# Three edits to a fused attention and feed-forward kernel: who adds up the probabilities and when, where GpSimd's bias goes, and a last tile in halves

## The chip, the cores and the metric

The kernel runs on one core of a Trainium2 chip. The metric is the device time of one execution in microseconds; the time of a kernel is the median of several runs. The engines are TensorE (PE, with its weight loads as PEld), VectorE (DVE), ScalarE (ACT), GpSimd (POOL) and SyncE (SP), which here only issues transfers.

## The reference

A block of a vision-language model for 4 batches of 512 tokens with 512 channels, and a context of 1024 tokens. Cut to what matters:

```python
def block(x, cond):                      # x (4,512,512), cond (4,1024,512)
    h = layernorm(x)
    q = qdq(h) @ qdq(wq).T + bq          # qdq: symmetric int8 rounding per row
    k, v = split(cond @ wkv.T + bkv)     # 16 heads of 32
    attn = softmax(q @ k.T / sqrt(32))
    o = attn @ v
    x = x + tanh(g_xattn) * (qdq(o) @ qdq(wp).T + bp)
    h = layernorm(x)
    f = silu(h @ gate_w * gs) * (h @ up_w * us)      # 1536 wide, weights fp8-rounded
    return x + tanh(g_ffn) * (f @ down_w * ds)
```

## The kernel before

All engines run their own written-out instruction lists and meet at semaphores. The kernel goes through the batches in four passes, b = 0 to 3.

The attention of a pass has 4 groups of 4 heads, and a group has 8 units, each of 128 context tokens for all 512 queries (`UNITS` is 32). A unit is: `scores` on TensorE (four matmuls, L1469), two exponentials on ScalarE (L836, two heads each), `values` on TensorE (four matmuls, L1486). The denominator of the softmax is a sum of the probabilities over all context tokens. In passes 1 to 3 the units named in `ADDED` (L157) are added up by VectorE (`add_unit`, two adds a unit, L1080) into `acc`; the first add of a group takes two units' probabilities, so seven units cost twelve adds. The units that are not named are summed by TensorE (`sums`, L1500). At the end of a group TensorE takes the finished `acc` in `totals` (L1514), which waits for the last add and stands in TensorE's list behind the first scores of the next group and ahead of all others. The next group's first add waits until `totals` has read `acc`. ScalarE may be three units ahead of the adds (`P_RING`).

Beside the adds VectorE prepares the next batch's x in steps, a generator `x_ahead` (L981) of which one step is taken ahead of the adds of each unit in `AHEAD_UNITS` (L136). Its order for passes 1 and on: four statistics (L958, one a tile), one aggregation (L964, L966), four normalisings (L969), four largest magnitudes (L935), the scales and four scalings (L944), four roundings (L950). `x_ahead(2)` runs in pass 1, `x_ahead(3)` in pass 2. The x itself is loaded at L536, when the gate and up products of the pass before are done.

GpSimd puts the bias of the projection on the residual in `residual_bias` (L666), four operations of 128x512; in passes 1 to 3 it does so behind the inverse deviation for the next x. VectorE wants the result ahead of the eviction of the projection (L1234).

Behind the attention ScalarE copies the denominator out of PSUM (L846, semaphore `den_out`) and the last group's output (L847). TensorE turns the denominator and the outputs; VectorE takes reciprocals (L1214) and multiplies (L1222, PSUM by `rden` into `r1`), finds magnitudes (L935), scales and rounds. Projection, second layernorm and the feed-forward part follow. In passes 0 and 1, steps for the next pass's score maxima are placed beside the down product: the last of them (`("S", G - 1, 0)`) stands ahead of the eviction of the last tile, `DOWN3`, and ends in VectorE's `crow` operation (L1047).

The down product has four tiles a pass. A tile is 24 matmuls of 512 columns (`down_step`, L1504); VectorE evicts it with the scale (L1155) and adds it to the residual (L1158, `down_tile`), and SyncE stores it (`store_rows`, L529). In the last pass nothing follows.

SyncE brings the stacked keys and queries of groups 2 and 3 (`stack`, 12 transfers each, L517, and `shift_row`, L527), started when the scores of the group before the last one are done.

Of the kernel before, what the change touches and what calls it, by code (L numbers as in the profile page):

```python
# [125 lines left out]
CHAIN_LATE = (CHAIN_LAST[0:5] + ["LATE1"] + CHAIN_LAST[5:13] + ["LATE2", "LATE3"] + CHAIN_LAST[13:])  # L126

LATE_EARLY = 8
D_SEQ = [CHAIN + HI_SEQ + ffn_seq(b) for b in range(B - 1)] + [CHAIN_LATE + ffn_seq(B - 1)]
D_BANK = [{n: k % 8 if k < len(CHAIN) else FREE_RING[(k - len(CHAIN)) % 4] for k, n in enumerate(seq)}  # L130
          for seq in D_SEQ[:B - 1]]
# [1 line left out]
_banks = (0, 1, 2, 3, 4, 5, 7, 0, 1, 2, 3, 4, 5, 7, 6)  # L133
D_BANK.append({n: _banks[k] if k < len(_banks) else (k + 1) % 8 for k, n in enumerate(D_SEQ[B - 1])})

AHEAD_UNITS = ((3, 5, 7, 18, 20) + tuple(range(22, 30)), tuple(range(1, 6)) + tuple(range(8, 25)))  # L136
STREAM0 = [s for n in A_SEQ0 for part in STEPS0.get(n, []) for s in part] + LEAD0 + UNIT_LIST0
assert [s for s in STREAM0 if s[0] == "D"] == DIFFS
STREAM0 = [s for s in STREAM0 if s[0] in "RSW"]
# [14 lines left out]
P_RING = (2, 3)  # L154


ADDED = ((0, 1, 2, 3, 4, 5, 6), (0, 1, 2, 4, 5, 6), (0, 1, 2, 4, 5, 6), (0, 1, 2, 3, 4, 5, 6))  # L157
ADD_HEADS = 2
ADD_PARTS = HG // ADD_HEADS
ADD_UNITS = [g * MT + t for g in range(G) for t in ADDED[g][1:]]  # L160
# [115 lines left out]
def pair_count(b, u, j):  # L276

    return b * 2 * UNITS + 2 * u + j // 2 + 1


class Steps:
# [14 lines left out]
def build(nc, ctxT, x, wq, wkvT, wp, gate_w, up_w, down_w, bqT, bkT, bv, bp, gsT, usT, ds,  # L296
          g_x, g_f, out):
    with ExitStack() as ctx:
# [177 lines left out]
        def _(sp):  # L476
# [52 lines left out]
            def store_rows(b, tiles):  # L529
                rows = out[b].rearrange("(t p) c -> p t c", p=P)  # L530
                for t in tiles:
                    sp.wait_ge(x_done, b * NT + t + 1)
                    sp.dma_start(rows[:, t, :], residual(b, t)).then_inc(stored, 16)

# [23 lines left out]
            for b in range(B):  # L558
# [43 lines left out]
                else:  # L602
                    store_rows(b - 1, LATE)
                    store_rows(b, range(NT))
            sp.wait_ge(stored, B * NT * 16)


        @block.gpsimd
        def _(pool):
# [32 lines left out]
            def inverse_deviation(n):  # L642
                pool.wait_ge(var_ready, n)
                nc.gpsimd.tensor_tensor(rstd[:, :], mv[:, :, 1], mhalf[:, :], ALU.pow).then_inc(rstd_ready, 1)  # L644
# [51 lines left out]
            for b in range(B):  # L696
                if b == 0:
                    first_units()
                else:
                    if b < B - 1:  # L700
                        inverse_deviation(variance_of_x(b + 1))
                    residual_bias(b)
                inverse_deviation(variance_of_x2(b))
                ahead = b + 2 < B
                if ahead:
                    pool.wait_ge(d_full, d_full_count(b, "K7"))
                    for c in range(CHUNK_BUFFERS[b + 2]):
                        load_ctx(b + 2, c)
                for i in range(FT):
                    pool.wait_ge(f_hi, b * FT + i + 1)  # L710
                    nc.gpsimd.tensor_tensor(f2_at(b, 1, i), fus[:, i % 2, :], f2_at(b, 0, i),  # L711
                                            ALU.subtract).then_inc(f_ready, 1)
                    if ahead and i in CHUNKS_BY_GATES[b]:
                        chunk(b + 2, CHUNKS_BY_GATES[b].index(i))
                for c in range(len(CHUNKS_BY_GATES[b]) if ahead else CHUNKS, CHUNKS):
                    chunk(b + 2, c)
# [188 lines left out]
        def _(dve):  # L905
# [277 lines left out]
            for b in range(B):  # L1183
                last = b == B - 1

                ahead = x_ahead(b + 1) if not last else None
                for u in range(UNITS):
                    g, t = divmod(u, MT)
                    if b == 0:
# [102 lines left out]
                    beside(name)  # L1292
                if b == 0:
                    dve.wait_ge(w_done, W_STEPS)
                for t in range(NT):
                    name = f"DOWN{t}"
                    if name not in d_seq(b):
                        continue
                    beside(name)
                    down_tile(b, t, b, name)  # L1300


        @block.tensor
        def _(pe):
# [196 lines left out]
                                          prob[:, p_slot(b, u, j), :], start=(u == (MT - 1 if b else 0)), stop=(u == UNITS - 1))  # L1501
                mm.then_inc(p_used, 1)

            def down_step(b, out, t, i):  # L1504
                for part in range(2):
                    mm = nc.tensor.matmul(out, f2_at(b, part, i)[:, t * P:(t + 1) * P], w_down[:, i, :],  # L1506
                                          start=(i == 0 and part == 0), stop=(i == FT - 1 and part == 1))
                return mm

# [59 lines left out]
            for b in range(B):  # L1569
# [23 lines left out]
                for name in d_seq(b):  # L1593
                    out_bank = d_bank(b, name)
                    out = bank(out_bank)
                    kind = name.rstrip("0123456789") if name[:3] != "X2T" else "X2T"
                    n = int(name[len(kind):] or 0)
                    if kind == "TOP":
                        continue
                    ahead = [lambda part=part: [maxima(b + 1, s) for s in part] for part in AHEAD[b].get(name, [])]  # L1600

                    if name != "LATE2":
                        bank_free(b, name)
                    if kind == "LATE":
                        for i in range(LATE_EARLY if n == 2 else 0, FT):
                            mm = down_step(b - 1, out, n, i)
                        mm.then_inc(d_full, 1)
                        if n == 1:
                            bank_free(b, "LATE2")
                            for i in range(LATE_EARLY):  # L1610
                                down_step(b - 1, bank(d_bank(b, "LATE2")), 2, i)
                    elif kind == "V":
                        if n == 0:
                            pe.wait_ge(ctx_ready, (b + 1) * CHUNKS)
                        v_product(out, n, d_full)
                    elif kind == "DEN":
                        pe.wait_ge(den_out, b + 1)
                        turn(out, [denT[:, t * P:(t + 1) * P] for t in range(NT)], d_full)
                    elif kind == "O":
                        if n == 0:  # L1620
                            pe.wait_ge(o_out, (b + 1) * G)
                        turn(out, [oT[:, g, n * P:(n + 1) * P] for g in range(G)], d_full)
                    elif kind == "OQT":
                        if n == 0:
                            pe.wait_ge(oq_ready, (b + 1) * NT)
                        turn(bank(out_bank, dt=BF16), [oq[:, t, n * P:(n + 1) * P] for t in range(NT)], d_full)
                    elif kind == "PROJ":
                        if n == 0:
                            pe.wait_ge(oqt_copied, (b + 1) * CT)
                        pair(out, [(oqT[:, k, n * P:(n + 1) * P], wpT[:, k, :]) for k in range(CT)], d_full)  # L1630
                    elif kind == "SX":
                        pe.wait_ge(diag_ready, (b + 2) * NT)
                        scales_product(out, d_full)
                    elif kind == "XT":
                        if n == 0:
                            pe.wait_ge(xq_ready, (b + 2) * NT)
                        turn_x(out_bank, n, d_full)
                    elif kind == "X2T":
                        if n == 0:
                            pe.wait_ge(x2_ready, (b + 1) * NT)  # L1640
                        turn(out, [x2[:, t, n * P:(n + 1) * P] for t in range(NT)], d_full)
                    elif kind == "Q":
                        if n == 0:
                            pe.wait_ge(x_copied, (b + 2) * X_COPIES)
                        q_product(out, n, d_full)
                    elif kind == "K":
                        k_product(out, n, d_full, ahead)
                    elif kind == "GU":
                        i, k = divmod(n, 2)
                        if n == 0:  # L1650
                            pe.wait_ge(d_free, d_free_count(b, f"X2T{CT - 1}"))
                        if b == 0 and i % (WCH // P) == 0:

                            pe.wait_ge(w_done, w_at[("gate", "up")[k], CT - 1, i // (WCH // P)] + 1)
                        pair(out, [((w_gate, w_up)[k][:, c, i * P:(i + 1) * P], x2T[:, s, c, :])
                                   for c in range(CT) for s in range(2)], d_full)
                        for step in ahead:
                            step()
                    else:
                        for i in range(FT):  # L1660
                            if ahead and i in (DOWN_AT_LATE if b == B - 2 else DOWN_AT)[name]:
                                ahead.pop(0)()
                            if n == 0:
                                if b == 0:
                                    pe.wait_ge(w_done, w_at["down", i] + 1)
                                pe.wait_ge(f_ready, b * FT + i + 1)
                            mm = down_step(b, out, n, i)
                        mm.then_inc(d_full, 1)
# [37 lines left out]
```

## Time and profile before

| | |
|---|---|
| median of 3 runs | 938.24 us (937.95 to 938.37) |
| the profiled execution | 936.7 us |
| its span, first to last instruction | 934.9 us, mean granted clock 0.991 |
| busy, share of the span | PE 92%, DVE 72%, ACT 59%, POOL 27% |
| chain that ended last | PE 68%, DVE 13%, ACT 10%, issue 7%, DMA 1% |
| load of x, 1024 KB | 6.0 us from issue to landing |

The span leaves out 1.8 us of the execution's time that lie around the instructions. Matmuls are pipelined in the trace: one that starts before the other ended is not a contradiction, and a busy TensorE is no measure of its peak. In the timelines, "x4" merges four operations of a kind; the time is from the start of the first to the end of the last; the bracket gives the idle time of the engine ahead of it and the engine and line that ended it.

### The profile page before, as it was taken

To read this page: it belongs to the slowest core of one execution; us is meant where nothing else is said; L and a number is where in the kernel's file an instruction comes from. 1 tells how busy PE (TensorE), PEld (TensorE's weight loads), DVE (VectorE), ACT (ScalarE), POOL (GpSimd) and SP (SyncE) were. 2 spreads that over 40 slices of the span, in tenths; PEclk is the share of its full clock that TensorE was granted. 3 is DMA by queue.
4 is the path that set the end of the run, shared out by engine and by line. 5 is a ranking of instruction groups with operands and counts; after the bars stand their busy time and mean duration, and the time that the engine had idled before them with its cause. 6 is when DMAs were issued, how large, how long until landed. Compare 5 with 4: busy or idle time off the path is not lost.

```text
span 934.9 us, 13575 instructions
## 1 busy us (share of the span) xinstructions
PE 864.1 (92%) x5000; PEld 310.2 (33%) x5000; DVE 671.5 (72%) x1292; ACT 554.4 (59%) x693; POOL 256.7 (27%) x236
## 2 busy tenths in 40 slices
PE   5987888999899998999899998999999989998998
PEld 2421121124433331224433331224433322233443
DVE  6887968938676769876766679886867768678222
ACT  5546777562556657884356647885256678871330
POOL 1145789770017603000006713000001213000130
PEclk9998999999999999999999999999999999999999
DMA  9334244410111143200020133210020014200001
GB/s 332 97 89 128 84 125 116 127 46 1 43 32 46 40 125 96 51 2 1 17 58 24 50 109 97 49 32 1 4 48 1 1 46 111 54 1 23 12 1 45
DMA packets 37106, 55.28 MB, mean 59 GB/s; under 512 B 8944, under 2 KB 15152, under 8 KB 37040
## 3 DMA queue, kind: packets, MB, share of 16 engines
q1 hardware_dynamic: 35120, 48.13, 18.1%
q0 software_dynamic: 1920, 6.29, 2.3%
q8 instruction: 39, 0.64, 0.3%
q14 instruction: 27, 0.22, 0.1%
HBM read 31.21 MB, written 4.19 MB: 38 GB/s over the span
## 4 chain that ended last, share of the span: by engine, by line
PE 68%; DVE 13%; ACT 10%; issue 7%; DMA 1%; ACTq 0%; DVEq 0%
PE ps L1325 33%; PE ps L1469 9%; PE ps L1506 8%; PE ps L1486 8%; ACT r L836 5%; PE ps L1448 4%; DVE acc L1080 3%; PE ps L1500 2%; PE ps L1514 1%; PE ps L1309 1%; DVE kst L1055 1%; ACT xq L795 1%; ACT r L795 1%; ACT r L744 1%; DVE r L1222 1%
## 5 line engine op out<-in xcount | busy, mean ns | idle before, releaser
L836 ACT ACTIVATE r<-ps 128x1024 f32<-128x1024 f32 x256 | 251.4, 1022 | 74.1 <-PE ps L1469 71.7
L1469 PE MATMUL ps<-qst,kst 97*128 97x512 f16 x512 | 140.9, 387 | 15.4 <-ACT r L836 13.0
L1055 DVE CUSTOM_DVE_ANT_0 kst<-ps,kst 128x512 f32<-128x512 f32 x192 | 124.5, 686 | 30.3 <-PE ps L1448 28.4
L1486 PE MATMUL ps<-r,vv 128*32 128x512 f32 x1024 | 138.1, 612 | 3.4 <-ACT r L836 3.2
L1080 DVE TENSOR_TENSOR acc<-acc,r 128x1024 f32<-128x1024 f32 x108 | 129.8, 1258 | 3.5 <-ACT r L836 3.1
L795 ACT ACTIVATE kst<-ps 128x1024 f32<-128x1024 f32 x96 | 98.2, 1023 | 53.3 <-PE ps L1381 53.0
L644 POOL TENSOR_TENSOR rstd<-mv,mhalf 128x4 f32<-128x4 f32 x8 | 9.9, 1240 | 344.9 <-DVE mv L966 344.9
L1325 PE MATMUL ps<-xs,w_gate 128*128 128x512 f16 x384 | 91.0, 380 | 1.5 <-DVE xs L1260 1.5
L1325 PE MATMUL ps<-xs,w_up 128*128 128x512 f16 x384 | 91.1, 380 | 0.0
L1469 PEld LDWEIGHTS ps<-qst,kst 97*128 97x128 f16 x512 | 37.6, 98 | 157.4 <-ACT r L836 110.7
L893 ACT ACTIVATE qst<-ps,gs_c 128x512 f32<-128x512 f32 x48 | 33.0, 688 | 67.7 <-PE ps L1325 67.7
L1289 DVE SCALAR_TENSOR_TENSOR xq<-ps,us_c,qst 128x512 f32<-128x512 f32 x48 | 36.0, 750 | 50.6 <-PE ps L1325 50.6
L1506 PE MATMUL ps<-w_down,r 128*128 128x512 f16 x288 | 66.1, 380 | 0.0
L1325 PE MATMUL ps<-ctx_hi,wkv_hi 128*128 128x512 f16 x128 | 49.1, 388 | 15.5 <-ACT ctx_hi L731 10.9
L711 POOL TENSOR_TENSOR r<-xq,r 128x512 f16<-128x512 f32 x36 | 42.6, 1182 | 71.5 <-ACT r L886 71.0
L1448 PE MATMUL ps<-k_reg,q_reg 32*128 32x512 f16 x256 | 49.9, 386 | 9.7 <-DVE mx L1055 7.1
L1080 DVE TENSOR_TENSOR acc<-r 128x1024 f32<-128x1024 f32 x24 | 29.3, 1263 | 34.7 <-ACT r L836 34.7
L1381 PE MATMUL ps<-acc,q_reg 32*128 32x512 f16 x256 | 49.9, 386 | 3.9 <-issue 2.8
L1500 PE MATMUL ps<-r,esel 128*32 128x512 f32 x400 | 52.8, 600 | 0.0
L1325 PEld LDWEIGHTS ps<-xs,w_gate 128*128 128x128 f16 x384 | 35.6, 98 | 46.7 <-issue 5.2
L1325 PEld LDWEIGHTS ps<-xs,w_up 128*128 128x128 f16 x384 | 34.6, 98 | 45.0 <-issue 8.2
L1325 PE MATMUL ps<-ctx_lo,wkv_hi 128*128 128x512 f16 x128 | 48.7, 385 | 0.3 <-DVE ctx_lo L1090 0.3
(164 smaller groups left out, 1322.1 us busy)
## 6 DMA issues: line engine op xcount, KB each, us to landing
kst<-k_reg SPq DMA_DIRECT2D x192, 64.0 KB
qst<-q_reg SPq DMA_DIRECT2D x192, 32.0 KB
xs<-in_x SPq DMA_DIRECT2D x4, 1024.0 KB, 6.0
cf<-in_ctxT POOLq DMA_DIRECT2D x16, 256.0 KB, 3.5
xres<-in_x SPq DMA_DIRECT2D x3, 1024.0 KB, 5.4
out<-xres SPq DMA_DIRECT2D x12, 256.0 KB, 2.1
acc<-in_down_w SPq DMA_DIRECT2D x10, 256.0 KB, 2.6
vv<-in_wkvT SPq DMA_DIRECT2D x2, 1024.0 KB, 9.8
```

Source lines behind the costliest of these rows:

```text
L711: nc.gpsimd.tensor_tensor(f2_at(b, 1, i), fus[:, i % 2, :], f2_at(b, 0, i), ALU.subtract).then_inc(f_ready, 1)
L795: nc.scalar.activation(kept(b, n), ps[:, first_bank:first_bank + 2, :], ACT.Relu, scale=2.0).then_inc(diff_kept, 1)
L836: nc.scalar.activation(prob[:, s:s + 2, :], ps[:, first_bank:first_bank + 2, :], ACT.Exp, scale=SCALE).then_inc(exp_done, 1)
L1055: ins = nc.vector.tensor_tensor_reduce(kept(b, n)[:, k, :], bank(PAIR + k), kept(b, n)[:, k, :], 1.0, -3.0e38, ALU.add, ALU.max, mx[:, g % ...
L1080: nc.vector.tensor_tensor(sums, other, prob[:, p:p + ADD_HEADS, :], ALU.add).then_inc(p_dve, 1)
L1325: mm = nc.tensor.matmul(out, l, r, start=(k == 0), stop=(k == len(terms) - 1))
L1381: mm = nc.tensor.matmul(bank(first_bank + k), qhi[rows, g, i // 2 * P:(i // 2 + 1) * P], kdiff[rows, g % 2, :], start=True, stop=True)
L1448: mm = nc.tensor.matmul(bank(PAIR + k), qhi[rows, g, t * P:(t + 1) * P], khi[rows, g, 512:1024], start=True, stop=True)
L1469: mm = nc.tensor.matmul(bank(first_bank + k), kst[0:97, g % 2, j + k, t * P:(t + 1) * P], qst[0:97, g % 2, j + k, :], start=True, stop=True)
L1486: mm = nc.tensor.matmul(ps[j * DH:(j + 1) * DH, O_BANK, :], vv[:, t, h * DH:(h + 1) * DH], prob[:, p_slot(b, u, j), :], start=(t == 0), st ...
L1500: mm = nc.tensor.matmul(ps[j * DH:(j + 1) * DH, DEN_BANK, :], esel[:, g, :], prob[:, p_slot(b, u, j), :], start=(u == (MT - 1 if b else 0) ...
L1506: mm = nc.tensor.matmul(out, f2_at(b, part, i)[:, t * P:(t + 1) * P], w_down[:, i, :], start=(i == 0 and part == 0), stop=(i == FT - 1 and ...
```

## The change

1. `ADDED` becomes units 0 to 6 in every group. Before, groups 1 and 2 left out unit 3, which TensorE summed. In passes 1 to 3 VectorE does two more adds in each of these two groups, and TensorE four matmuls (as eight records) less.
2. The first four steps of `x_ahead(2)` and `x_ahead(3)`, the statistics, move from units 1 to 4 of passes 1 and 2 to the end of passes 0 and 1: two ahead of the last `S` step beside `DOWN3`, two behind its eviction. The aggregation moves from unit 5 to unit 3. The other steps stay at units 8 to 24.
3. GpSimd's `residual_bias(b)` in passes 1 to 3 waits for `den_out` of its own pass.
4. `DOWN3` of the last pass is computed, evicted, added and stored in two halves of 256 columns, the second half in another bank (that of `DOWN1`).

```diff
-AHEAD_UNITS = ((3, 5, 7, 18, 20) + tuple(range(22, 30)), tuple(range(1, 6)) + tuple(range(8, 25)))
+AHEAD_UNITS = ((3, 5, 7, 18, 20) + tuple(range(22, 30)), (3,) + tuple(range(8, 25)))
+AHEAD_EARLY = (2, 2)
-ADDED = ((0, 1, 2, 3, 4, 5, 6), (0, 1, 2, 4, 5, 6), (0, 1, 2, 4, 5, 6), (0, 1, 2, 3, 4, 5, 6))
+ADDED = (tuple(range(MT - 1)),) * G
+LAST_BANK = D_BANK[B - 1][f"DOWN{NT - 3}"]
+def last_cols(half):
+    return slice(half * C // LAST_PARTS, (half + 1) * C // LAST_PARTS)
...
+                    if b == B - 1 and t == NT - 1:
+                        for half in range(LAST_PARTS):
+                            sp.wait_ge(x_done, b * NT + t + 1 + half)
+                            sp.dma_start(rows[:, t, last_cols(half)], residual(b, t)[:, last_cols(half)]
+                                         ).then_inc(stored, 16)
+                        continue
...
+                    pool.wait_ge(den_out, b + 1)
                     residual_bias(b)
...
+                ahead = x_ahead(b + 2) if b + 2 < B else None
                 for t in range(NT):
...
-                    beside(name)
+                    for part in AHEAD[b].get(name, []):
+                        if part == [("S", G - 1, 0)] and ahead:
+                            for _ in range(AHEAD_EARLY[0]):
+                                next(ahead)
+                        maxima(b + 1, part)
+                    if last and t == NT - 1:
+                        continue
                     down_tile(b, t, b, name)
+                if last:
+                    dve.wait_ge(x_done, B * NT - 2)
+                    for half in range(LAST_PARTS):
+                        cols, at = last_cols(half), bank(d_bank(b, f"DOWN{NT - 1}") if half == 0 else LAST_BANK)
+                        dve.wait_ge(d_full, d_full_count(b, f"DOWN{NT - 1}") + half)
+                        nc.vector.tensor_tensor(down[:, 1, cols], at[:, cols], ds_bc[:, cols], ALU.mult).then_inc(d_free, 1)
+                        dve.wait_ge(d_free, d_free_count(b, f"DOWN{NT - 1}") + half)
+                        rows = residual(b, NT - 1)[:, cols]
+                        nc.vector.tensor_tensor(rows, rows, down[:, 1, cols], ALU.add).then_inc(x_done, 1)
+                for _ in range(AHEAD_EARLY[1] if ahead else 0):
+                    next(ahead)
...
+                    if last and kind == "DOWN" and n == NT - 1:
+                        released(b, f"DOWN{NT - 3}")
...
+                    elif last and n == NT - 1:
+                        for half in range(LAST_PARTS):
+                            for i in range(FT):
+                                mm = down_step(b, out if half == 0 else bank(LAST_BANK), n, i, last_cols(half))
+                            mm.then_inc(d_full, 1)
```

## Rows read from the trace of the kernel before

**Rows 1.** Stretches, first add to first add: busy PE, PEld, DVE, ACT, POOL; clock; DMA.

```profile
346.68:368.00 21.32, 17.89 (x112) 4.29 (x112) 20.95 (x24) 16.03 (x18) 9.09 (x5) 0.96 0.34 100
368.00:387.62 19.62, 19.62 (x128) 4.53 (x120) 16.24 (x20) 15.98 (x18) 0.00 (x0) 0.96 0.20 46
387.62:405.92 18.30, 18.30 (x124) 4.51 (x120) 13.77 (x16) 15.99 (x18) 0.00 (x0) 1.00 0.21 50
766.82:784.24 17.42, 17.42 (x116) 4.25 (x112) 13.71 (x13) 15.92 (x18) 6.40 (x4) 1.00 0.42 119
```

**Rows 2.** Timeline, end of pass 1's first group: start us, duration us, operations, [idle before].

```profile
358.05 6.79 DVE L1080 TENSOR_TENSOR acc<-acc,r 128x1024 f32<-128x1024 f32 x4
...
360.16 7.22 POOL L669 TENSOR_TENSOR xres<-xres,bp_bc 128x512 f32<-128x512 f32 x4
...
364.89 1.06 PE L1514 MATMUL ps<-acc,esel 128*32 128x512 f32 x8 [3.43 <-DVE acc L1080]
```

**Rows 3.** Busy times in one microsecond behind that wait; clock third from last.

```profile
367.00:368.00 1.00, 1.00 (x6) 0.20 (x8) 0.67 (x2) 1.00 (x2) 0.37 (x1) 0.50 0.53 125
```

**Rows 4.** Timeline of TensorE, two other idle times, in the last pass.

```profile
850.90 3.61 PE L1325 MATMUL ps<-wpT,r 128*128 128x512 bf16 x16 [1.56 <-ACT r L864]
...
863.98 3.21 PE L1309 MATMUL ps<-identf,r 128*128 128x128 f32 x16 [2.56 <-DVE r L969]
```

**Rows 5.** Timeline of VectorE, all adds of pass 1's fourth group.

```profile
405.92 2.36 DVE L1080 TENSOR_TENSOR acc<-r 128x1024 f32<-128x1024 f32 x2 [4.34 <-ACT r L836]
...
408.20 11.44 DVE L1080 TENSOR_TENSOR acc<-acc,r 128x1024 f32<-128x1024 f32 x10
```

**Rows 6.** Timeline of VectorE, three steps of x and the adds behind them.

```profile
398.56 0.42 DVE L950 TENSOR_SCALAR xs<-xs 128x512 f32<-128x512 f32 x1
398.89 1.22 DVE L1080 TENSOR_TENSOR acc<-acc,r 128x1024 f32<-128x1024 f32 x1
...
587.69 0.54 DVE L969 TENSOR_SCALAR xs<-xs,mv,rstd 128x512 f32<-128x512 f32 x1
588.15 1.22 DVE L1080 TENSOR_TENSOR acc<-acc,r 128x1024 f32<-128x1024 f32 x1
...
591.00 0.69 DVE L935 TENSOR_REDUCE am<-xs 128x1 f32<-128x512 f32 x1
591.60 1.22 DVE L1080 TENSOR_TENSOR acc<-acc,r 128x1024 f32<-128x1024 f32 x1
```

**Rows 7.** Timeline, end of pass 0: load of x, crow, last down tile's add.

```profile
326.01 0.58 SPq L536 DMA_DIRECT2D xs<-in_x  x1
...
341.54 0.68 DVE L1047 TENSOR_SCALAR crow<-ps 4x512 f16<-4x512 f32 x1 [1.68 <-PE ps L1403]
...
343.99 0.69 DVE L1158 TENSOR_TENSOR xres<-xres,acc 128x512 f32<-128x512 f32 x1
```

**Rows 8.** Timeline, last pass: last transfer of the third group's stack, and its scores.

```profile
793.96 0.64 SPq L527 DMA_DIRECT2D qst<-crow  x1
...
797.00 1.04 PE L1469 MATMUL ps<-qst,kst 97*128 97x512 f16 x4
```

**Rows 9.** Timeline behind the attention: pass 1 (421, 425), pass 0 (204, 207).

```profile
204.19 4.96 POOL L669 TENSOR_TENSOR xres<-xres,bp_bc 128x512 f32<-128x512 f32 x4
...
207.97 0.69 DVE L1147 TENSOR_TENSOR vv<-ps,bv_bc 128x512 f32<-128x512 f32 x1 [6.21 <-PE ps L1325]
...
421.69 0.59 ACT L846 COPY r<-ps 128x512 f32<-128x512 f32 x1 [3.16 <-PE ps L1500]
...
425.58 2.48 DVE L1222 TENSOR_TENSOR r<-ps,rden 128x512 f32<-128x512 f32 x4
```

**Rows 10.** Timeline of the end of the kernel.

```profile
931.76 0.69 DVE L1158 TENSOR_TENSOR wkv_lo<-wkv_lo,acc 128x512 f32<-128x512 f32 x1
...
932.48 0.33 SPq L533 DMA_DIRECT2D out<-wkv_lo  x1
```

**Rows 11.** Busy times while the last store moves; share of the DMA engines last but one.

```profile
933.00:934.00 1.00, 0.00 (x0) 0.00 (x0) 0.00 (x0) 0.00 (x0) 0.00 (x0) 1.00 0.67 254
```

More of the change, by code:

```diff
@@ L128 @@
 LATE_EARLY = 8
+LAST_PARTS = 2
 D_SEQ = [CHAIN + HI_SEQ + ffn_seq(b) for b in range(B - 1)] + [CHAIN_LATE + ffn_seq(B - 1)]
@@ L604, in _ @@
                     store_rows(b, range(NT))
-            sp.wait_ge(stored, B * NT * 16)
+            sp.wait_ge(stored, (B * NT + LAST_PARTS - 1) * 16)
         @block.gpsimd
@@ L1184, in _ @@
                 last = b == B - 1
-                ahead = x_ahead(b + 1) if not last else None
+                if b == 0:
+                    ahead = x_ahead(1)
                 for u in range(UNITS):
@@ L1502, in sums, with down_step @@
                 mm.then_inc(p_used, 1)
-            def down_step(b, out, t, i):
+            def down_step(b, out, t, i, cols=slice(0, C)):
                 for part in range(2):
-                    mm = nc.tensor.matmul(out, f2_at(b, part, i)[:, t * P:(t + 1) * P], w_down[:, i, :],
+                    mm = nc.tensor.matmul(out[:, cols], f2_at(b, part, i)[:, t * P:(t + 1) * P], w_down[:, i, cols],
                                           start=(i == 0 and part == 0), stop=(i == FT - 1 and part == 1))
```

## The prediction

> **What bounds the kernel now.** I read the granted clock first (0.99 of full over the span, so the clock is a matter of single spots), then the chain that ended last, then the stretches between two first adds of a group, then the timelines of VectorE, GpSimd and TensorE around the places that the change touches. A pass of the attention has four head groups of eight units. TensorE and ScalarE go through a unit side by side; VectorE adds up the probabilities behind them, and at the end of a group TensorE needs the finished sum for `totals`. I measure a group from its first add (the one that writes `acc` from the probabilities alone) to the next group's.
>
> [rows 1] are four such stretches. The first group of the last pass, where VectorE has nothing but its adds and nobody waits, takes 17.42 us. The third group of pass 1 takes 18.30: one unit more is summed by TensorE, 0.88 us. The same 18.30 is there three times (pass 1's third group, the last pass's second and third). The first group of pass 1 takes 21.32 and its second 19.62. [rows 2] say why: two of the adds at its end lose their pace (four adds take 6.79 us) while GpSimd puts the bias on the residual (four operations in 7.22 us), and `totals` starts at 364.89 after an idle of 3.43 us, 0.05 after the last add. Behind that idle the granted clock is 0.50, 1.2 GHz [rows 3], and this runs on into the second group. Pass 2 shows the same two groups with the same sum; the last pass has no such wait.
>
> **The adds with their steps.** Twelve adds, back to back from the first one, last 13.72 us [rows 5] (405.92 to 419.64). A step of the next batch's x between two adds costs the difference of the starts: normalising 0.46 us, the largest magnitude 0.60, the rounding 0.33 [rows 6]; the scaling isn't in the rows, I take 0.4, between them.
>
> From the start of `totals` to the next first add there are 3.11 us in pass 1 (364.89 to 368.00), about 0.3 of which I put down to the halved clock (estimate, two score matmuls at half speed); at the full clock 2.82. So a group takes the larger of 17.42 and of VectorE's time + 0.05 + 2.82. The two meet where VectorE has 14.55 us of work.
>
> **Passes 1 and 2, first group.** The four statistics leave it: two go ahead of the last maxima of the pass before, two behind the last down tile. There VectorE sits idle for 1.68 us ahead of the crow operation [rows 7], and a statistic reads 512 columns of one tile as the magnitude does, a slot of 0.60 [rows 6]. The other two, 1.2 us, fit between the down tile's add, ended at 344.68 [rows 7], and the first attention add at 346.68 [rows 1]. The x that they read was asked for at 326.01 [rows 7], 13 us before they want it, over twice its landing time (6.0 us in the page's list of DMA issues). Were it late, crow, the last down tile and the scores behind would wait. The bias leaves the group as well. What is left is 13.72 and one aggregation (0.5 us, estimated as one bare slot like those of [rows 6]), 14.2, under 14.55: 17.42 us, where the rows have 21.32.
>
> **Passes 1 and 2, second group.** Now VectorE adds unit 3 of the group too, and TensorE loses 0.88 us of sums. But five steps of x stand between the first and the last add: two normalisings and three magnitudes, 0.92 + 1.80 = 2.72. VectorE has 16.44, over 14.55 by 1.9. The group takes 16.44 + 2.87 = 19.31, against 19.62 now (and against 18.30 if now had no halved clock in it). So here the larger share of adds costs more than TensorE's sums did, and a new wait of TensorE on the last add appears, 1.7 us of idle matmul time (3.43 idle belongs to a lateness of 4.0 by the same count).
>
> **Passes 1 and 2, third group.** Two scalings, three roundings, 1.8 us: 13.72 + 1.8 + 2.87 = 18.39 against 18.30. A wait of a microsecond or less, and no gain.
>
> Pass 1: 21.32 + 19.62 + 18.30 = 59.24 becomes 17.42 + 19.31 + 18.39 = 55.12, -4.1 us; pass 2 the same, -4.1. The fourth groups keep their units and adds.
>
> **Last pass.** No x is prepared there, so in the second and third group 13.72 lies under 14.55 and both take 17.42 for 18.30: -1.8 us. What comes late next is SyncE's stack: its last transfer is issued at 793.96, and the scores that need it start at 797.00 [rows 8], with the change at 796.1. An output store, the nearest row for a landing, needs at most 2.4 us from its issue to the end of the span [rows 10], which would be 796.4. So 0.3 us is the bound there, in two groups, and 0 what I take, as the crow rows are 4 KB and the store 256.
>
> **The bias behind the denominator.** GpSimd now starts when ScalarE's copy of the denominator ends (421.69 + 0.59), and needs 4.96 us undisturbed [rows 9], to 427.3. Queued behind it on GpSimd are the inverse deviation and the next context loads, wanted much later. VectorE in this time does the denominator's reciprocals and the four products of 425.58 to 428.06, on the chain. All of these read PSUM. The nearest rows: GpSimd's four bias operations of pass 0 with a VectorE operation out of PSUM in the midst, 0.69 us as everywhere [rows 9]. I take 0, with the bounds 0 and 4.96 a pass.
>
> The Trainium skill, "SBUF — State Buffer", "Who interferes with whom", says that GpSimd shares one SBUF port pair with VectorE, held by whoever came first, and that a VectorE instruction with at most one SBUF input and outside the two-port modes doesn't take part. By that rule the products (one PSUM, one SBUF input) go free and the adds (two SBUF inputs) don't. [rows 2] and [rows 9] agree with it on both sides. By its price of a full block the cost would be the upper bound above for adds, and 0 for this place.
>
> **The tail.** TensorE's part is 24 matmuls of 512 columns, now 48 of 256, and each still needs its weights loaded. At the pace of the sixteen of [rows 4] the 24 take 5.2 us; half the columns twice is the same. I add 0.06 for issue; bounds 0 and 0.3. Behind the last matmul lie the product with the scale and the add, 0.69 us each [rows 10]. An add of 1024 elements takes 1.22 [rows 6], so 256 elements less are 0.27 less: two times, -0.53. The first half's two operations and its store lie beside the second half's matmuls. The last store moves 128 KB instead of 256: the DMA engines were busy for 0.67 us for the whole [rows 11], half would be 0.33, but the packets become half as long and not fewer; I take 0.2, bounds 0 and 0.35. The wait of TensorE on the second bank is on a tile evicted 4 us earlier. Sum -0.7 us, between -0.3 and -0.9.
>
> The Trainium skill, "DMA: Bandwidth & Descriptors", "Anatomy of one DMA", gives a fixed 2.0 us and the bytes at 436 GB/s. By it the half store would save 0.3 us, for my 0.2, and the whole store would take 2.6, where [rows 10] leave 2.4 from the issue to the end of the span.
>
> **The sum.** -4.1 - 4.1 - 1.8 - 0.7 = -10.7 us. The profiled execution took 936.7 us (span 934.9 and 1.8 around it), so 926.0; the median of the three runs, 938.24, lies 1.5 over it, so I forecast 927.5. Some 0.2%, 1.9 us, is what a measurement of this kernel tells from no change.
>
> **Rivals.**
> - The clock falls behind the new wait of the second groups. The rows have a fall after an idle of 2.56 us (16 transposes then take 3.21) and none after 1.56 (16 matmuls at full pace, 3.61) [rows 4]; mine is 1.7, nearer the second. Price: 1.32 us (19.62 less 18.30) and 0.3, in two passes: 3.2 us, time 930.7.
> - VectorE hides its steps better than by these slots, or the adds run closer. With no waits at all all groups take 17.42: 5.7 us more, 921.8. Halfway, 924.7, is the likelier form. Against it: in [rows 5] VectorE's adds leave no gap to fill.
> - Slower than before: the bias, at its new place, blocks VectorE's reciprocals and products. It is on the chain in three passes. At the full 4.96 us each that is 14.9, time 942.4; it decides from 3.6 us a pass. Against it [rows 9]; and in passes 1 and 2 the reductions behind the products start only after GpSimd's end (428.06 against 427.3). In the last pass, where no product of values stands between, they would meet its last microsecond. A small collision, 1 us a pass, gives 930.5.
> - The change doesn't do what it says: the first group's wait stays because something else is late (x not landed, the aggregation held up). Then half of 8.2 is gone: 931.6 to 933.
>
> **Chances.** The forecast 0.55; the clock 0.17; better hidden steps 0.13; small collision 0.06; wait kept 0.04; slower 0.05. From 924.8 to 931.2 lie the forecast, the clock, the small collision and part of the third. Faster by over 0.2%: 0.93; within 0.2%: 0.02; slower: 0.05.
>
> **What would show it.** First groups of passes 1 and 2 of 17.4 us with no idle ahead of `totals`; second groups of 19.3 with an idle of 1.7 us put down to the last add, and the clock at 1.00 behind it; third groups of 18.4; in the last pass 17.4 three times. Bias operations of 1.24 us each behind the denominator's copy and products that still take 0.62 us apiece. At the end two short operations of 0.42 us. The forecast is wrong if the steps' slots differ under the longer queue of adds, if an idle of 1.7 us costs the clock, or if products out of PSUM slow down beside GpSimd.

## The result and the profile after

The changed kernel takes 927.23 us in the median of 4 runs (926.27 to 928.09), the kernel before beside it 938.31 (937.95 to 938.67): a ratio of 0.9883, 95% interval 0.9869 to 0.9897. The profiled execution took 926.46 us with a span of 924.7.

The stretches of [rows 1] after the change, from one first add to the next; the columns are those of [rows 1]. The first two lines are pass 1's second and third group, the third is pass 2's first and the last is the last pass's second:

```profile
364.51:383.81 19.30, 17.64 (x116) 4.16 (x112) 18.23 (x22) 16.00 (x18) 0.00 (x0) 1.00 0.28 66
383.81:402.23 18.42, 17.66 (x116) 4.16 (x112) 15.85 (x19) 15.99 (x18) 0.00 (x0) 1.00 0.20 46
559.36:576.78 17.42, 17.42 (x116) 4.25 (x112) 15.10 (x20) 15.91 (x18) 1.89 (x1) 1.00 0.37 105
776.45:793.90 17.45, 17.45 (x116) 4.26 (x112) 13.72 (x13) 15.99 (x18) 0.00 (x0) 1.00 0.29 69
```

In the third and fourth line TensorE is busy for the whole stretch; in the first it lacks 1.66 us. The timeline of that group's end shows why (start us, duration us, engine, line, operation, [idle before, what ended it]):

```profile
377.96 0.68 DVE L953 TENSOR_REDUCE am<-xs 128x1 f32<-128x512 f32 x1
378.56 2.35 DVE L1098 TENSOR_TENSOR acc<-acc,r 128x1024 f32<-128x1024 f32 x2
...
380.96 1.07 PE L1551 MATMUL ps<-acc,esel 128*32 128x512 f32 x8 [1.66 <-DVE acc L1098]
...
383.81 2.36 DVE L1098 TENSOR_TENSOR acc<-r 128x1024 f32<-128x1024 f32 x2 [0.97 <-ACT r L854]
```

The two last adds end at 380.91, `totals` starts 0.05 later, and 2.85 us after that the next group's first add. The granted clock behind this idle is 1.00, 2.4 GHz. [rows 2] had 3.43 us of idle in the group before it; that one is gone.

Where the 10.2 us of span went, stage by stage, from the copy of the denominator and the first exponential of each pass in the two traces:

| stretch | before | after | difference |
|---|---|---|---|
| start to pass 1's first exponential | 343.70 | 344.06 | +0.36 |
| attention of pass 1 | 77.99 | 73.92 | -4.07 |
| attention of pass 2 | 77.95 | 73.88 | -4.07 |
| attention of the last pass | 72.76 | 71.04 | -1.72 |
| between the attentions, two stretches | 138.39, 125.80 | 138.39, 125.80 | 0.00 |
| from the last pass's denominator to its down product | 73.52 | 73.58 | +0.06 |
| down product to the end | 24.78 | 23.98 | -0.80 |

The first row's difference is there already at pass 0's copy of the denominator (205.30 and 205.67), ahead of everything that the change touches. No run shows where it comes from.

The bias at its new place, and what VectorE does beside it, in pass 1 and (the last three lines) in the last pass:

```profile
418.64 4.96 POOL L686 TENSOR_TENSOR xres<-xres,bp_bc 128x512 f32<-128x512 f32 x4 [64.09 <-ACT r L864]
...
421.87 2.48 DVE L1241 TENSOR_TENSOR r<-ps,rden 128x512 f32<-128x512 f32 x4
...
827.75 4.96 POOL L686 TENSOR_TENSOR wkv_lo<-wkv_lo,bp_bc 128x512 f32<-128x512 f32 x4 [79.01 <-ACT r L864]
...
829.05 2.48 DVE L1241 TENSOR_TENSOR r<-ps,rden 128x512 f32<-128x512 f32 x4
...
831.57 2.46 DVE L953 TENSOR_REDUCE am<-r 128x1 f32<-128x512 f32 x4
```

GpSimd takes the undisturbed 4.96 of [rows 9], VectorE's four products the 2.48 of [rows 9], and the reductions that meet GpSimd's last microsecond 2.46 as elsewhere.

The end, which answers to [rows 10]: VectorE's timeline, and from the list of DMA issues the stores (count, KB each, us from issue to landing):

```profile
921.65 0.42 DVE L1332 TENSOR_TENSOR acc<-ps,ds_bc 128x256 f32<-128x256 f32 x1 [1.67 <-PE ps L1543]
922.11 0.42 DVE L1335 TENSOR_TENSOR wkv_lo<-wkv_lo,acc 128x256 f32<-128x256 f32 x1
```

```profile
out<-wkv_lo SPq DMA_DIRECT2D x3, 256.0 KB, 2.0
out<-wkv_lo SPq DMA_DIRECT2D x2, 128.0 KB, 1.7
```

### The profile page after: what moved, and what is told of

It reads as the page before. It is cut to its first block, busy times and chain, and to the rows that moved or that the text cites. A ratio compares the mean times of both kernels' runs of the same rounds, so it can differ in the third digit from the quotient of the medians.

```text
span 924.7 us, 13556 instructions
## 1 busy us (share of the span) xinstructions
PE 855.6 (93%) x4968; PEld 310.5 (34%) x4976; DVE 675.5 (73%) x1306; ACT 554.0 (60%) x693; POOL 249.7 (27%) x236
## 4 chain that ended last, share of the span: by engine, by line
PE 65%; DVE 14%; ACT 13%; issue 7%; DMA 1%; ACTq 0%; DVEq 0%
PE ps L1362 33%; ACT r L854 9%; PE ps L1543 8%; PE ps L1506 7%; PE ps L1523 7%; PE ps L1485 4%; DVE acc L1098 4%; PE ps L1551 1%; PE ps L1537 1%; PE ps L1346 1%; DVE kst L1073 1%; DVE am L953 1%; ACT xq L813 1%; ACT r L813 1%; ACT r L762 1%
## 5 line engine op out<-in xcount | busy, mean ns | idle before, releaser
L1098 DVE TENSOR_TENSOR acc<-acc,r 128x1024 f32<-128x1024 f32 x120 | 138.6, 1215 | 0.0
L1543 PE MATMUL ps<-w_down,r 128*128 128x512 f16 (+1 forms) x312 | 66.2, 363 | 0.0
L686 POOL TENSOR_TENSOR xres<-xres,bp_bc 128x512 f32<-128x512 f32 x12 | 14.9, 1271 | 128.5 <-ACT r L864 128.5
L1362 PE MATMUL ps<-wkv_lo,ctx_hi 128*128 128x512 f16 x128 | 48.6, 380 | 0.0
```

Source lines behind the costliest of these rows:

```text
L1098: nc.vector.tensor_tensor(sums, other, prob[:, p:p + ADD_HEADS, :], ALU.add).then_inc(p_dve, 1)
L1362: mm = nc.tensor.matmul(out, l, r, start=(k == 0), stop=(k == len(terms) - 1))
L1543: mm = nc.tensor.matmul(out[:, cols], f2_at(b, part, i)[:, t * P:(t + 1) * P], w_down[:, i, cols], start=(i == 0 and part == 0), stop=(i = ...
```

## The experiments

The theory is the prediction's: in passes 1 and 2 a group takes the larger of 17.42 us (TensorE and ScalarE) and of VectorE's time from first to last add + 2.87; what GpSimd and the steps of x take from VectorE there is all that counts, and adds are worth something only where VectorE has room. The rival is that each part pays by itself. The table has the stretches that the traces show, in us, for the first, second and third group of each pass; "before" was timed beside each set of experiments, and its medians are given as a range.

| kernel | median us | pass 1 | pass 2 | last pass |
|---|---|---|---|---|
| before | 937.64 to 938.46 | 21.32, 19.62, 18.30 | 22.36, 18.55, 18.30 | 17.42, 18.29, 18.30 |
| changed | 927.23 | 17.12, 19.30, 18.42 | 17.42, 19.31, 18.41 | 17.42, 17.45, 17.44 |
| adds only | 937.48 | 22.35, 20.08, 18.41 | 22.36, 19.30, 18.42 | 17.42, 17.61, 17.44 |
| bias only | 930.50 | 18.90, 18.30, 18.30 | 18.90, 18.30, 18.30 | 17.42, 18.30, 18.30 |
| adds undone | 926.68 | 17.12, 18.30, 18.30 | 17.42, 18.30, 18.30 | 17.42, 18.30, 18.30 |
| bias undone | 937.81 | 22.01, 19.45, 18.42 | 21.67, 19.31, 18.41 | 17.42, 17.60, 17.44 |
| statistics undone | 930.72 | 18.89, 19.31, 18.42 | 18.90, 19.31, 18.41 | 17.42, 17.45, 17.44 |
| steps between groups | 920.88, 921.56 | 17.12, 17.44, 17.44 | 17.42, 17.48, 17.44 | 17.42, 17.45, 17.44 |
| the same, adds undone | 927.24 | 17.12, 18.30, 18.30 | 17.42, 18.30, 18.30 | 17.42, 18.30, 18.30 |

**The adds alone**, in the kernel before.

```diff
-ADDED = ((0, 1, 2, 3, 4, 5, 6), (0, 1, 2, 4, 5, 6), (0, 1, 2, 4, 5, 6), (0, 1, 2, 3, 4, 5, 6))
+ADDED = (tuple(range(MT - 1)),) * G
```

> The kernel before with the adds alone moved to VectorE (six units, twelve adds more; TensorE six times 0.88 us less). Theory A (VectorE's time sets these groups in passes 1 and 2): first groups of passes 1 and 2 keep their wait, their second groups come to 19.3 to 19.7 us and their third to 18.4, nothing gained there; only the last pass gains, 1.5 us. Time 937 to 938. Rival B (TensorE's sums lie on the chain in all three passes, so each is worth 0.88): -5.3 us, 933.

Measured 937.48 us (10 runs), ratio 0.9992 with an interval of 0.9974 to 1.0011: nothing. The last pass gains 1.5 us, and the three groups of passes 1 and 2 together take 1.6 and 0.9 more, a longer fall of the clock in pass 1 among it. Rival B's 0.5% is outside the interval.

**The bias alone**, in the kernel before.

```diff
+                    pool.wait_ge(den_out, b + 1)
                     residual_bias(b)
```

> The kernel before with the bias behind the denominator alone. Theory A (GpSimd's bias slows VectorE's adds, which end the first groups): first group = 13.72 + four statistics and an aggregation 2.5 + 2.87 = 19.1 us for 21.3, idle ahead of totals 1.5 and no fall of the clock, so the second group takes 18.3 for 19.6: -3.5 us in each of passes 1 and 2, time 931.3. Rival B (the statistics alone make the wait): idle stays near 3.4, time 938. Rival C (the bias collides behind the attention): slower than 938.

Measured 930.50 us, ratio 0.9920 (0.9888 to 0.9951). First groups of 18.90, second ones of 18.30 in both passes. The first groups are 0.2 us shorter than expected because only three of the four statistics lie behind the first add, which takes two units' probabilities: 13.72 + 3 x 0.60 + 0.5 + 2.87 = 18.9. The idle ahead of `totals` is 1.27 us and the clock keeps 1.00:

```profile
363.86 1.06 PE L1515 MATMUL ps<-acc,esel 128*32 128x512 f32 x8 [1.27 <-DVE acc L1081]
```

So one line of the change is worth 7.5 us by itself, where the whole change is worth 11. Rivals B and C fall.

**The adds undone**, in the changed kernel: `ADDED` as before.

> The changed kernel with the adds undone (TensorE sums unit 3 of groups 1 and 2 again). Theory A: second and third groups of passes 1 and 2 take 18.3 each instead of 19.30 and 18.42, with no wait on VectorE (-1.1 us a pass), the last pass's two take 18.3 for 17.4 (+1.7): 926.7, the same as the changed kernel. Rival B (the adds pay in every pass): +5.3 us, 932.5.

Measured 926.68 us (925.52 to 927.78) beside the changed kernel's 927.23 (926.27 to 928.09). No idle ahead of any `totals` is left in its trace. In the changed kernel the adds are worth nothing in sum: 1.72 us gained in the last pass, 2 x 1.1 lost in the two others.

**The bias undone**, in the changed kernel.

```diff
-                    pool.wait_ge(den_out, b + 1)
                     residual_bias(b)
```

> The changed kernel with the bias back behind the inverse deviation (the wait on the denominator taken out). Theory A: the bias starts in the fourth unit, lies wholly beside the adds and takes 2.5 to 4 us from VectorE: first groups of passes 1 and 2 of 19.5 to 20.5 us for 17.1, an idle time ahead of totals of 2 us or more, perhaps a fall of the clock: 932 to 936 us. Rival B (with the statistics gone the bias costs nothing): 927.

Measured 937.81 us (10 runs), ratio 0.9995 (0.9979 to 1.0011): the whole gain is gone, and that is more than I expected (932 to 936). With the statistics gone GpSimd is ready for the bias earlier, waits there for the load of the residual, and then has its four operations wholly beside the adds. In pass 1:

```profile
356.47 8.37 POOL L686 TENSOR_TENSOR xres<-xres,bp_bc 128x512 f32<-128x512 f32 x4 [1.89 <-DMA xres<-in_x]
...
352.46 13.47 DVE L1097 TENSOR_TENSOR acc<-acc,r 128x1024 f32<-128x1024 f32 x8
...
365.98 0.64 PE L1550 MATMUL ps<-acc,esel 128*32 128x512 f32 x4 [4.14 <-DVE acc L1097]
```

The four operations take 8.37 us against 4.96 undisturbed, and the eight adds beside them 13.47 against 9.17 in the changed kernel: 4.3 us, where my range went to 4. In pass 2 the bias starts later by 1.1 us, the eight adds take 12.42, and the idle is 2.74. Behind both idles, 4.14 and 2.74, the clock falls to 0.50, which I had called possible.

**The statistics undone**, in the changed kernel: all steps of `x_ahead` in units 1 to 5 and 8 to 24 as before.

> The changed kernel with the four statistics back in the first group. Theory A: 13.72 + 2.5 + 2.87 = 19.1 us for 17.1 to 17.4 in the first groups of passes 1 and 2, idle of 1.5 us ahead of totals, no fall of the clock: +1.8 us each, 931. Rival B (only the bias made the wait): 927.

Measured 930.72 us, ratio 0.9912 (0.9888 to 0.9936). First groups of 18.9, an idle of 1.27 and no fall of the clock there. The statistics are worth 1.5 (pass 2) to 1.8 us (pass 1) once the bias is away.

**The steps between the groups**, in the changed kernel. The wait that the changed kernel has left (19.30, 18.42) should be the steps of x between first and last add. Here they are taken several at a time in the pause that VectorE has between a group's last add and the next one's first: five behind the first group, four behind the second (the text below says five) and the other seven behind the third.

```diff
-AHEAD_UNITS = (..., (3,) + tuple(range(8, 25)))
+AHEAD_UNITS = (..., (3, 7, 7, 8, 8, 9, 15, 15, 16, 17, 23, 23, 23, 24, 24, 25, 25))
-                    if not last and u in AHEAD_UNITS[b > 0]:
+                    for _ in range(0 if last else AHEAD_UNITS[b > 0].count(u)):
                         next(ahead, None)
```

> The changed kernel, with the steps of the next x in passes 1 and 2 taken out from between the adds: five at the end of each of the groups 0 and 1, the rest at the end of group 2, in the idle time of VectorE between last add and next first add. Theory A: VectorE's time falls to 13.72 in the second and third groups, under 14.55, all groups take 17.4, -1.9 and -1.0 in two passes: 921.5 us, no wait ahead of totals. Rival B (the wait seen there has another owner, or the steps now delay the first adds): 925 to 928.

Measured 920.88 us (920.02 to 921.53), ratio 0.9816 (0.9789 to 0.9844), and once more on another occasion, at 921.56:

> The kernel with the steps of x between the groups once more, as the base for the next one on the same chip. Both theories: 920 to 922 us, in two clusters some 1.3 us apart, as the clock's fall behind the idle of 2.56 us in the last pass (ahead of the transposes of the second layernorm's output) lasts longer in some runs than in others.

VectorE's timeline of pass 1's second group: five steps ahead of its first add, then twelve adds in a row.

```profile
362.03 1.91 DVE L988 TENSOR_SCALAR xs<-xs,mv,rstd 128x512 f32<-128x512 f32 x4
363.98 0.69 DVE L954 TENSOR_REDUCE am<-xs 128x1 f32<-128x512 f32 x1
365.02 2.36 DVE L1099 TENSOR_TENSOR acc<-r 128x1024 f32<-128x1024 f32 x2 [0.35 <-ACT r L855]
367.29 11.44 DVE L1099 TENSOR_TENSOR acc<-acc,r 128x1024 f32<-128x1024 f32 x10
```

and its stretch, in which TensorE has no gap:

```profile
365.02:382.46 17.44, 17.44 (x116) 4.25 (x112) 16.33 (x19) 15.99 (x18) 0.00 (x0) 1.00 0.28 66
```

**The same with the adds undone.**

> The changed kernel with the steps of x between the groups and the adds undone. Theory A: TensorE is the bound in all groups; each unit summed by it costs 0.88 us again, six of them, so 5.3 us more than with all adds on VectorE and the same steps: 926.8 if that one takes 921.5. Rival B: the sums are hidden in part, 924 or less.

Measured 927.24 us (927.22 to 927.48), 6.4 more than the 920.88 of the kernel with all adds; 5.1 of them are in the stretches of the table (six times 0.82 to 0.86). The two were not timed on the same chip, and 1.0 of the difference lies behind the last pass's attention, where the clock's fall was longer in this trace (below). So a unit's adds are worth nearly all of TensorE's 0.88 us as soon as no step stands in their way.

Beside "adds undone" (926.68) this run says one thing more: the steps' new place alone is worth nothing either, since the stretches of the two are the same. With the rest of the change in place, the kernel takes 926.68 us with neither of the two, 927.23 with the adds alone, 927.24 with the steps' new place alone and 920.88 with both.

**The last tile alone**, in the kernel before: part 4 of the change.

> The kernel before with only the last tile in halves. Theory A: 0.76 us less, as the two traces show from the start of the down product to the end: 0.54 by the two shorter operations of VectorE, 0.3 by the shorter store, 0.06 given back by TensorE. Time 937.5. Rival B: the store's landing is not shortened in the runs, -0.5 or nothing.

Measured 937.12 us against 937.64, ratio 0.9991, interval 0.9975 to 1.0007. The medians leave the sign open, as the runs of each kernel spread over 5 us. The stretch from the down product to the end shows it, 24.78 to 24.00 us. The runs show it too if they are sorted by their mean granted clock, which was done afterwards: on this chip the means are 940.33 before and 939.71 with the halves at 0.987, 938.42 and 937.99 at 0.989, 936.89 and 935.92 at 0.991, 935.18 and 934.60 at 0.993, so 0.4 to 1.0 us less at each level (one to nine runs behind each mean).

**A longer wait.** One reduction more in pass 1's second group, two more in pass 2's; their results go nowhere.

```diff
+                    for k in range(b if 0 < b < B - 1 and u == MT + 4 else 0):
+                        nc.vector.tensor_reduce(small[:, 40 + 2 * b + k:41 + 2 * b + k], vv[:, 0, :], AX.X, ALU.max)
```

> The changed kernel with one more reduction of 0.6 us among the steps of pass 1's second group and two more in pass 2's (their results are not used), so that TensorE's idle ahead of totals becomes 2.26 us and 2.86 us for 1.66. Theory A (the clock falls behind idles somewhere between 1.66 and 2.6 us): pass 2's group falls to 0.50 for some microseconds and costs 1.2 + 1.3 or more, pass 1's is open; time 930 to 933. Rival B (the length of the idle doesn't decide): only the 1.8 us of the reductions, 929.0, clock 1.00 in both.

Measured 930.51 us (928.74 to 932.15). In the trace, behind an idle of 2.25 us in pass 1 the clock stays at 1.00 and the group takes 19.89, 0.59 more. Behind 2.75 in pass 2 it falls, and the group takes 21.34, 2.03 more for 1.2 us of reductions:

```profile
595.37 1.49 PE L1553 MATMUL ps<-acc,esel 128*32 128x512 f32 x8 [2.75 <-DVE acc L1098]
```

One microsecond of each (clock third from last): 384 to 385 behind the shorter idle, 597 to 598 behind the longer. The falls differ between executions: the four runs' mean granted clocks go from 0.989 (932.15 us) to 0.994 (928.74).

```profile
384.00:385.00 1.00, 1.00 (x9) 0.15 (x8) 0.23 (x1) 1.00 (x2) 0.00 (x0) 1.00 0.16 40
597.00:598.00 1.00, 1.00 (x3) 0.30 (x2) 0.24 (x1) 0.06 (x1) 0.00 (x0) 0.50 0.37 87
```

**Matmuls in the idle of the last pass**, on top of the steps between the groups. This idle ahead of the transposes is the 2.56 us of [rows 4].

```diff
                     elif kind == "X2T":
+                        if n == 0 and last:
+                            for _ in range(8):
+                                nc.tensor.matmul(out, wpT[:, 0, 0:P], wpT[:, 1, :], start=True, stop=True)
```

> The same, and in the last pass TensorE does eight matmuls that nobody reads (0.216 us each, 1.7 us) ahead of its wait for the second layernorm's output, so that the idle of 2.56 us there becomes 0.8. Theory A (the fall of the clock there costs 0.8 or 2.1 us, by its length): clock 1.00 throughout the stretch, 0.8 to 2.1 us less than the base, and a narrower spread of the runs: 919 to 919.5. Rival B (the clock falls there for another reason, or the matmuls delay the transposes): the same as the base or slower.

Measured 919.95 us; the four runs are 919.79, 919.93, 919.97 and 922.19, those of its base on the same chip 919.38, 921.42, 921.70 and 921.98. In the trace the idle is 0.74, the transposes take 1.97 us, the clock is 1.00, and from the denominator's copy to the down product there are 72.68 us against the base's 73.77. The 1.6 us between the two medians isn't safe: each kernel has a run at the other's level. The mean granted clock sorts these eight runs: it is 0.996 in three runs with the matmuls (919.79 to 919.97) and in one of the base (919.38), and 0.994 in the four others (921.42 to 922.19). At the same clock the matmuls save nothing; at most they make the fall rarer, and four runs of each don't show that. The narrower spread that I expected didn't come. The median of 919.95 is the lowest of the study.

## Why the prediction was right

- **First groups.** 17.42 us was forecast for both; pass 2 has it. In pass 1 the first add itself came 0.35 us later behind the first exponential than before (3.33 us for 2.98), so the stretch shows 17.12; counted from the first exponential both passes gain the same 4.07. The wait is gone, as is the clock's fall. "The bias alone" and "the statistics undone" show that both parts are needed, and that the first is the larger.
- **Second groups**, forecast 19.31, measured 19.30 and 19.31; idle 1.7, measured 1.66; 2.82 us from `totals` to the next first add, measured 2.85. That VectorE would go over its 14.55 us there, and that this part of the change costs more than it gives, was the least certain of the steps, and the experiments confirm it from both sides: without the adds 18.30, with the steps out of the way 17.44.
- **Third groups**, forecast 18.39, measured 18.42 and 18.41.
- **Last pass**, forecast -1.8, measured -1.72. The stack was no wait.
- **The bias behind the denominator**, taken at 0 between 0 and 4.96: 0.00 in both stretches between the attentions. The Trainium skill ("SBUF — State Buffer", "Who interferes with whom") says that a VectorE instruction with at most one SBUF input keeps out of GpSimd's way; that holds here on the products (2.48 us) and on the reductions (2.46). Its other half, that two SBUF inputs bring a VectorE add into the way of a GpSimd instruction that reads SBUF, is what "the bias undone" shows at 4.3 us.
- **The tail**, forecast -0.7, measured -0.80 in the traces: -0.54 by VectorE, as forecast; -0.3 by the store, where I had taken 0.2; +0.06 by TensorE, as forecast. The Trainium skill ("DMA: Bandwidth & Descriptors", "Anatomy of one DMA") gives its 2.0 us and 436 GB/s for transfers that GpSimd issues; these stores are SyncE's, which the prediction doesn't say. By that fit they would take 2.6 and 2.3 us, an estimate. The saving of 0.3 agrees with the measured 2.0 to 1.7; the fixed part is too large here for both.
- **The sum**, forecast -10.7, measured -10.2 in the span; 0.36 of the difference lies ahead of pass 1.
- **The last step, from the profiled execution to the median**, was luck in part. The forecast of 927.5 carries over the 1.5 us by which the median before lay above its profiled execution. After the change that distance is 0.8 (927.23 and 926.46). The saving was taken 0.5 us too large and this distance 0.7 too large; the first makes the forecast too short, the second too long, and 0.3 us is left.

The rival with the falling clock stayed away: behind the idle of 1.66 the clock kept 1.00 in all four places (pass 1 and pass 2, here and in "the statistics undone"), and in the one trace of "a longer wait" behind 2.25 too. Its mechanism is real, but its price was too high: 0.83 us in the one case that fell there, where I had 1.6.

## What to carry to other kernels

Before work is moved to an engine that runs behind another, add up what that engine does between its first and its last deadline, small side jobs included: here 14.55 us was the limit, 13.72 were the adds, and 2.7 us of side steps turned a gain of 0.88 into a loss of 1.0. Put the side steps into the pauses between the deadlines and move the work, both together: each alone gave nothing here, and the pair some 6 us. An edit that measures as worthless may be waiting for another one. And keep GpSimd's operations on SBUF out of a stretch of VectorE adds whose end somebody waits for: one added wait on GpSimd was worth 7.5 us by itself, more than all the rest.

## What the runs showed of the hardware

- After the same idle of 2.56 us of TensorE in the last pass the clock isn't always the same. In twelve traces with that idle the stretch from the denominator's copy to the down product takes 72.75 us (once: the clock stays at 1.00), 73.5 to 73.8 (four times: some four microseconds at or near 0.50) or 74.8 (seven times: some seven). With the matmuls put in it takes 72.68. Two of them, the bias alone and the adds alone, TensorE's timeline:

```profile
857.63 1.94 PE L1310 MATMUL ps<-identf,r 128*128 128x128 f32 x16 [2.56 <-DVE r L970]
```

```profile
865.85 2.52 PE L1309 MATMUL ps<-identf,r 128*128 128x128 f32 x16 [2.56 <-DVE r L969]
869.87 1.01 PE L1325 MATMUL ps<-xs,w_gate 128*128 128x512 f16 x2 [1.49 <-DVE xs L1260]
```

  In the second the matmuls of the gate start at half speed, two in 1.01 us. Whether this makes the two clusters of the changed kernel's runs (926.27 and 926.46, 927.99 and 928.09) isn't shown: one of the four was traced, and the granted clocks on record, 0.994 three times and 0.993 for 927.99, don't separate them.
- Over the traces the idles of TensorE and the clock behind them line up like this: 1.00 behind 1.27 and 1.66 (two traces each, four places each) and 2.25 (once); 1.00 once and 0.50 eleven times behind 2.55 to 2.56; 0.50 behind 2.74, 2.75, 3.43 and 4.14.
- The spread of the runs goes with the length of the falls. The kernel before was timed 43 times beside the experiments, on three chips, from 935.11 to 940.67 us. Sorted by the run's mean granted clock these times fall into bands that don't overlap: 935.1 to 935.3 us at 0.993, 936.4 to 937.6 at 0.991, 937.9 to 938.7 at 0.989 and 0.990, 940.0 to 940.7 at 0.987. "The adds alone" and "the last tile alone" spread as widely and over as many levels; "the bias undone" has only 0.987 and 0.989 in its ten runs and stays within 1.8 us. So a difference of a microsecond between such kernels is best read at equal granted clock, unless the edit changes the falls themselves. Why an execution gets the longer or the shorter falls stays open.
- GpSimd's bias and VectorE's adds beside each other on SBUF cost both, in "the bias undone": 8.37 us for 4.96 on the one, 13.47 for 9.17 on the other.
